# A quantised weight product and a feed-forward layer on one core: each codebook level summed in two 512-column halves, row products issued singly

## The chip, the core and the metric

The kernel runs on one core of one Trainium2 chip. The metric is the device time of one execution in microseconds (us).

## The reference

`x` is 4096 tokens (32 tiles of 128) by 2048. A weight matrix (2048 by 2048) is quantised with a codebook of 32 sorted entries, with a low-rank delta inside and outside the quantiser:

```python
lora_delta = lora_B @ lora_A * (LORA_ALPHA / LORA_RANK)        # rank 64
cb = codebook / jnp.clip(jnp.max(jnp.abs(codebook)), 1e-08)
normalized = ((weight + lora_delta).reshape(O, I // 128, 128)) / scale
idx = jnp.searchsorted((cb[:-1] + cb[1:]) * 0.5, normalized, side='left')
w_eff = (cb[idx] * scale).reshape(O, I) + lora_delta
c = x @ w_eff.T
result = jnp.einsum('bsd,od->bso', c, W_base) + b_base         # then a routed low-rank term
return x + result + mixed_term
```

The kernel multiplies the two weight matrices first (G = w_eff.T @ W_base.T, with 24 more columns for the router and the low-rank term, and the identity added for the residual) and then x @ G.

## The kernel before

**Tiles and groups.** The quantised matrix is worked on as 32 tiles q, each 128 partitions by 1024 columns, in buffers `wr`. Two tiles give one block of G's 16 row blocks, and four blocks make a group. The startup makes tiles 0 to 7, the first group. Then TensorE streams x through that group (`chunk`), makes the next group's G from tiles prepared meanwhile (`slot`), and so on. In this later part the work on tiles 8 to 31 goes on as background of ScalarE, VectorE and GpSimd, level by level between the evacuations.

**One tile.** The codebook has 31 steps. For each of them a mask is made by ScalarE (`ACT.Identity` with a huge scale, saturating into uint8: 0 or 255). For 24 levels (unit(q, j), j = 0 to 23) the mask `mk` is summed by VectorE into `acc`, which lies in PSUM over two banks; each sum reads the `acc` that the one before wrote and so waits for its end (semaphore `ac`). For the 7 other levels the mask `mp` goes to GpSimd, which scales it into `tm` (L1302) and adds it into `pp` (L1315). The places of these seven in ScalarE's order are j = 0, 1, 3, 6, 10, 13, 16 in the startup. The first level subtracts the normalised weight in `acc` (L1111), and GpSimd's first add starts from the same weight, so it cancels. VectorE closes the tile into `wr` (L1122, semaphore `cl`), GpSimd scales it and adds the delta (`effective`, L1323 and L1325, semaphore `we`). GpSimd also normalises the next tile (L1288, L1291). There are five mask buffers, so ScalarE can run five levels ahead of VectorE.

**TensorE in the startup.** When a tile is effective, its rows of G are summed by eight row products of five matmuls each (L703, fp32), each with one row tile of W_base that SP loads into three buffers (L511); the load for a product waits for the product three before it. `rows(q - 1)` issues the eight in one piece behind unit(q, 7). Delta products (L682 and L683) for coming tiles go through the single PSUM bank `pd`: each waits until the one before has been copied out to `ds` (semaphore `dl`), by ScalarE (L906) in unit order, the first four by VectorE (L1099). Places of delta products are `DELTA_AT`, a table of (q, j); there are 64, of which 36 lie in the startup. After tile 7 `final` multiplies its rows in another way (L722 on), after which the first `chunk` follows at once. At unit(q, 3) of tiles 3, 5, 7 `rows_out` copies the finished block of G (five ScalarE copies L957, five VectorE subtractions L1149).

**What sets the order.** `walk()` is one list of events. Each engine's program walks it and issues its own part of every event in that order; engines are bound to each other by semaphores alone. SP walks it too: a load or store that waits holds all that SP issues behind it.

Of the kernel before, what the change touches and what calls it, by code (L numbers as in the profile page):

```python
# [15 lines left out]
H = D // 2  # L16
# [64 lines left out]
def startup():  # L81
    for q in range(2 * N0):
        for j in range(NV):
            yield ("unit", q, j)
            if j == 7 and q:
                yield ("rows", q - 1)
            if j == 3 and q >= 3 and q % 2:
                yield ("rows_out", (q - 3) // 2)
# [110 lines left out]
class Room:  # L199
    def __init__(self, nc, ctx):  # L200
# [52 lines left out]
        self.dj = self.take("dj", NJ)  # L253
        self.sm = self.take("sm", 2)
# [109 lines left out]
def on_vector(n):  # L364

    return n < 4
# [7 lines left out]
def mask_places(q):  # L374

    return FIRST_AT if q == 0 else EARLY_AT if q < 2 * N0 else SPARE_AT

# [60 lines left out]
def book_steps(e, R, S):  # L438
# [17 lines left out]
    yield e.tensor_scalar(th, th, 0.5, None, ALU.mult).then_inc(bk, 1)  # L456
    yield e.tensor_tensor(dj, cn[:, 1:NC], cn[:, 0:NJ], ALU.subtract).then_inc(bk, 1)
    e.wait_ge(bk, 9)
# [16 lines left out]
BOOK_READY = 23  # L475


def sync_program(e, R, S, io, part, delta, out):
# [105 lines left out]
    for ev in walk():  # L584
# [17 lines left out]
        elif what == "rows":  # L602
            for r in range(8 * at[0] + 3, 8 * at[0] + 11):
                row(r)
            if at[0] == 2 * N0 - 3:
# [53 lines left out]
def tensor_program(e, R, S):  # L659
# [32 lines left out]
    def rows(q):  # L692
        b, h = q // 2, q % 2
        e.wait_ge(S["we"], q + 1)
        if q == 0:
            e.wait_ge(S["dl"], NARROW)
        for t in range(8 * h, 8 * h + 8):
            r = NB * b + t
            e.wait_ge(S[f"r{r % 3}"], 16 * (r // 3 + 1))
            for c in range(NCH):  # L700
                if t == 0 and b:
                    e.wait_ge(S["lo"], NCH * (b - 1) + c + 1)
                done = e.matmul(R.m[c][:, 0:width(c)], R.wr[raw_of(q)][:, (t % 8) * 128:(t % 8 + 1) * 128],  # L703
                                R.rows[r % 3][:, cols(c)], start=t == 0, stop=t == NB - 1 and not own(b, c))
            done.then_inc(S["row"], 1)
        if h:
# [129 lines left out]
    def turn(t):  # L836
# [3 lines left out]
        else:  # L840
            e.wait_ge(S["cl"], NQ)
# [12 lines left out]
    for ev in walk():  # L854
# [4 lines left out]
        elif what == "rows":  # L859
# [594 lines left out]
```

## Time and profile before

| | |
|---|---|
| device time, three runs | 2389.73 us median (2389.25 to 2390.38) |
| the profiled execution | span 2389.1 us from first to last instruction; its time is not listed apart from the three |
| TensorE, VectorE, ScalarE, GpSimd busy | 97%, 71%, 60%, 53% of the span |
| startup, until the first product of x | 339.1 us |

Busy time is an average over stages. The stages are told apart by windows, and what ends a wait by the rows of the timeline: a row's start, its duration, and in brackets how long the engine was idle ahead of it and for whom. Several alike instructions in a row are merged (x20), and their duration is that of the whole run; the time from one start to the next start is called the pitch here.

### The profile page before, as it was taken

The numbers are of one execution on the slowest core, as the hardware profiler recorded it, in microseconds if no ns is written. First come the engines' busy times: TensorE is split into PE (matmuls) and PEld (weight loads), VectorE is DVE, ScalarE is ACT, GpSimd is POOL, SyncE is SP. The second block draws the span as 40 slices with busy tenths as digits, with TensorE's granted clock in tenths as the row PEclk, the third lists the DMA queues.
The fourth block names the chain that finished last, engine by engine and source line by source line (L and its number), as shares of the span: only waits on it lengthen the run. The fifth ranks groups of instructions, "written<-read, shape, count | busy, mean of one in ns | idle before, by whom it ended". The sixth has DMA issues, their size and how long they took to land.

```text
span 2389.1 us, 30759 instructions
## 1 busy us (share of the span) xinstructions
PE 2318.9 (97%) x11678; PEld 2102.9 (88%) x11678; DVE 1708.0 (71%) x2021; ACT 1427.1 (60%) x1799; POOL 1270.6 (53%) x704
## 2 busy tenths in 40 slices
PE   3989899999999999999999999999999999999999
PEld 2445479999999999999999999999999989999998
DVE  8899998999978868777868967878873333333333
ACT  7999978989977656665646657566643321111111
POOL 6989847779874437777764436777760000111010
PEclk9989999999999999999999999999999999999999
DMA  5788854443343435766764436667664334545554
GB/s 198 272 274 277 309 208 162 162 166 141 138 149 114 118 116 197 238 230 225 234 219 123 119 105 200 222 232 238 221 208 128 102 96 161 197 180 198 185 195 152
DMA packets 121561, 442.58 MB, mean 185 GB/s; under 512 B 12818, under 2 KB 53330, under 8 KB 84562
## 3 DMA queue, kind: packets, MB, share of 16 engines
q1 hardware_dynamic: 121412, 440.61, 54.4%
q8 instruction: 92, 1.51, 0.3%
q14 instruction: 57, 0.47, 0.1%
HBM read 289.43 MB, written 151.13 MB: 184 GB/s over the span
## 4 chain that ended last, share of the span: by engine, by line
PE 91%; DVE 4%; ACT 3%; POOL 1%; issue 0%; DMA 0%; SPq 0%; DVEq 0%; POOLq 0%; ACTq 0%
PE m L777 20%; PE m L776 20%; PE m L778 20%; PE m L761 8%; PE m L762 8%; PE m L760 8%; PE m L703 4%; DVE acc L1115 3%; ACT mk L918 2%; PE m L806 1%; ACT mp L924 1%; PE pd L682 0%; DMA lb<-in_lb 0%; PE pd L683 0%; ACT ds L906 0%
## 5 line engine op out<-in xcount | busy, mean ns | idle before, releaser
L1115 DVE SCALAR_TENSOR_TENSOR acc<-mk,dj,acc 128x1024 f32<-128x1024 uint8 x736 | 944.9, 1284 | 91.6 <-ACT mk L918 72.1
L776 PE MATMUL m<-gh,xh 128*128 128x384 f32 (+2 forms) x2560 | 903.2, 353 | 0.0
L777 PE MATMUL m<-gl,xh 128*128 128x384 f32 (+2 forms) x2560 | 898.7, 351 | 0.0
L778 PE MATMUL m<-gh,xl 128*128 128x384 f32 (+2 forms) x2560 | 896.0, 350 | 0.0
L918 ACT ACTIVATE mk<-wr,bj 128x1024 uint8<-128x1024 f32 x768 | 843.8, 1139 | 0.7 <-DVE acc L1115 0.7
L776 PEld LDWEIGHTS m<-gh,xh 128*128 128x128 f32 x2560 | 481.6, 188 | 23.5
L778 PEld LDWEIGHTS m<-gh,xl 128*128 128x128 f32 x2560 | 480.9, 188 | 23.6
L777 PEld LDWEIGHTS m<-gl,xh 128*128 128x128 f32 x2560 | 481.4, 188 | 21.2
L1315 POOL TENSOR_TENSOR pp<-pp,tm 128x1024 f32<-128x1024 f32 x192 | 466.4, 2429 | 22.0
L1335 POOL TENSOR_TENSOR xl<-xw,xh 128x512 fp32r<-128x512 f32 x96 | 124.1, 1294 | 564.7 <-ACT xh L972 564.4
L1302 POOL TENSOR_SCALAR tm<-mp,dj 128x1024 f32<-128x1024 uint8 x224 | 258.1, 1152 | 246.5 <-ACT mp L924 235.6
L760 PE MATMUL m<-kh,wh 128*128 128x384 f32 (+2 forms) x936 | 328.8, 351 | 0.0
L762 PE MATMUL m<-kh,wl 128*128 128x384 f32 (+2 forms) x936 | 328.2, 351 | 0.0
L761 PE MATMUL m<-kl,wh 128*128 128x384 f32 (+2 forms) x936 | 328.0, 350 | 0.0
L1169 DVE TENSOR_TENSOR kl<-kw,kh 128x384 fp32r<-128x384 f32 (+2 forms) x234 | 189.1, 822 | 141.2 <-ACT kh L952 140.7
L1163 DVE TENSOR_TENSOR part<-m,part 128x384 f32<-128x384 f32 (+2 forms) x320 | 187.9, 587 | 131.5 <-PE m L778 130.4
L952 ACT ACTIVATE kh<-kw 128x384 fp32r<-128x384 f32 (+2 forms) x234 | 126.8, 548 | 251.8 <-DMA kw<-in_wb 251.2
L924 ACT ACTIVATE mp<-wr,bj 128x1024 uint8<-128x1024 f32 x224 | 255.1, 1139 | 0.1
L972 ACT ACTIVATE xh<-xw 128x512 fp32r<-128x512 f32 x128 | 80.1, 628 | 240.2 <-DMA xw<-in_x 240.2
L703 PE MATMUL m<-rows,wr 128*128 128x384 f32 (+2 forms) x560 | 207.6, 534 | 2.3 <-POOL wr L1325 1.5
L703 PEld LDWEIGHTS m<-rows,wr 128*128 128x128 f32 x560 | 112.2, 201 | 96.3 <-issue 50.6
L760 PEld LDWEIGHTS m<-kh,wh 128*128 128x128 f32 x936 | 175.8, 188 | 8.4 <-POOL wl L1329 0.2
(131 smaller groups left out, 1781.3 us busy)
## 6 DMA issues: line engine op xcount, KB each, us to landing
part<-part SPq DMA_DIRECT2D x192, 1036.0 KB, 6.7
rows<-in_wb SPq DMA_DIRECT2D x61, 1036.0 KB, 4.8
xw<-in_x SPq DMA_DIRECT2D x128, 256.0 KB, 3.2
out<-part SPq DMA_DIRECT2D x31, 1024.0 KB, 4.2
kw<-in_wb SPq DMA_DIRECT2D x138, 192.0 KB, 2.4
wr<-in_w SPq DMA_DIRECT2D x32, 512.0 KB, 8.8
dl<-delta SPq DMA_DIRECT2D x30, 512.0 KB, 5.9
delta<-ds SPq DMA_DIRECT2D x24, 512.0 KB, 3.2
```

Of the source, the lines that this page charges most:

```text
L703: done = e.matmul(R.m[c][:, 0:width(c)], R.wr[raw_of(q)][:, (t % 8) * 128:(t % 8 + 1) * 128], R.rows[r % 3][:, cols(c)], start=t == 0, sto ...
L760: e.matmul(bank[:, 0:w], high, kh, start=t == 0, stop=False)
L761: e.matmul(bank[:, 0:w], high, kl, start=False, stop=False)
L762: done = e.matmul(bank[:, 0:w], low, kh, start=False, stop=t == NB - 1 and not own(b, c))
L776: e.matmul(R.m[c][:, 0:w], xh, gh, start=k == 0, stop=False)
L777: e.matmul(R.m[c][:, 0:w], xh, gl, start=False, stop=False)
L778: done = e.matmul(R.m[c][:, 0:w], xl, gh, start=False, stop=stop and k == n - 1)
L918: e.activation(R.mk[k % NM], w, ACT.Identity, bias=R.bj[:, j:j + 1], scale=GROW).then_inc(S["mk"], 1)
L924: e.activation(R.mp[k % 2], w, ACT.Identity, bias=R.bj[:, NV + i:NV + i + 1], scale=GROW).then_inc(S["mp"], 1)
L1115: e.scalar_tensor_tensor(R.acc, R.mk[k % NM], R.dj[:, j:j + 1], R.acc, ALU.mult, ALU.add).then_inc(S["ac"], 1)
L1302: e.tensor_scalar(R.tm[scaled_level(q, i)], R.mp[k % 2], R.dj[:, NV + i:NV + i + 1], 0.0, ALU.mult, ALU.add).then_inc(S["tm"], 1)
L1315: e.tensor_tensor(R.pp, R.pp if i else R.wr[raw_of(q)], R.tm[scaled_level(q, i)], ALU.add).then_inc(S["pp"], 1)
```

## The change

Each level is summed in two halves of 512 columns, one instruction each, where a half waits only for the same half of the level before. The first level is no longer masked by ScalarE: VectorE compares the normalised weight itself (`is_gt`) and multiplies by the first codebook step. The weight no longer enters `acc` and `pp`; GpSimd's first mask is scaled with the lowest codebook entry added, and its next add starts from two `tm`, which makes six adds for seven. The tile is closed in two halves. `effective` waits for the close itself and no more for the first level of the next tile.

The eight row products become eight events behind units 7, 10, 15, 17, 20, 23, 23, 23 and the delta products of tiles 3 to 7 stand behind units 9, 14, 19, 23. The second and fourth of them are copied out by VectorE, the others by ScalarE. Tile 1 now has eight delta products (six before), tile 2 none (two before).

```diff
@@ -25,9 +25,12 @@
 NJ = NC - 1
 NP = 7
 NV = NJ - NP
+NA, MK = NP - 1, NV - 1
+HALVES = (slice(0, H // 2), slice(H // 2, H))
 SPARE_AT = (0, 3, 6, 10, 13, 16, 19)
 FIRST_AT, EARLY_AT = (1, 3, 5, 8, 11, 14, 17), (0, 1, 3, 6, 10, 13, 16)
 NORM_AT, SPLIT_EVERY = 8, 6
+ROW_AT, LATE_UNITS = (7, 10, 15, 17, 20, 23, 23, 23), (9, 14, 19, 23)
 GROUP = (4, 4, 4, 4)
 FINAL_ROW = NB * GROUP[0] - NB // 2
 CUT = (0, 384, 768, 1152, 1664, DX)
...
@@ -345,8 +350,8 @@
 
 def delta_places():
 
-    late = [(0, j) for j in range(6, 22, 2)] + [(1, j) for j in range(1, 7)] + [(2, 3), (2, 4)]
-    late += [(q, j) for q in range(3, 2 * N0) for j in range(3, 7)]
+    late = [(0, j) for j in range(6, 22, 2)] + [(1, j) for j in (1, 2, 3, 4, 5, 6, 9, 14)]
+    late += [(q, j) for q in range(3, 2 * N0) for j in LATE_UNITS]
     late += [(q, j) for q in range(2 * N0, NQ) for j in range(5, NV, 3)]
     return dict(zip(late, range(NDELTA)))
 
@@ -363,7 +368,7 @@
 
 def on_vector(n):
 
-    return n < 4
+    return n < 4 or 16 <= n < 16 + 4 * (2 * N0 - 3) and n % 2 == 1
 
 
 def unit_at(n):
...
@@ -599,10 +610,9 @@
-        elif what == "rows":
-            for r in range(8 * at[0] + 3, 8 * at[0] + 11):
-                row(r)
+        elif what == "row":
+            row(8 * at[0] + 3 + at[1])
...
@@ -908,14 +918,15 @@
                      scale=0.5).then_inc(S["dl"], 1)
 
     def unit(q, j):
-        k, w = NV * q + j, R.wr[raw_of(q)]
+        m, w = MK * q + j - 1, R.wr[raw_of(q)]
         if j == 0:
             e.wait_ge(S["n"], q + 1)
             if q == 0:
                 e.wait_ge(S["bk"], BOOK_READY)
-        if k >= NM:
-            e.wait_ge(S["ac"], k - NM + 1)
-        e.activation(R.mk[k % NM], w, ACT.Identity, bias=R.bj[:, j:j + 1], scale=GROW).then_inc(S["mk"], 1)
+        else:
+            if m >= NM:
+                e.wait_ge(S["ac"], summed((m - NM) // MK, (m - NM) % MK + 1))
+            e.activation(R.mk[m % NM], w, ACT.Identity, bias=R.bj[:, j:j + 1], scale=GROW).then_inc(S["mk"], 1)
         if j in mask_places(q):
             i = mask_places(q).index(j)
             k = NP * q + i
...
@@ -1100,32 +1111,36 @@
     def unit(q, j):
-        k = NV * q + j
-        if q >= 2 * N0 or k == 0:
-            e.wait_ge(S["mk"], k + 1)
-        elif j % 2:
-            e.wait_ge(S["mk"], k + 1 + (j < NV - 1))
-        if j == 0:
-            if q:
-                e.wait_ge(S["cl"], q)
-            e.scalar_tensor_tensor(R.acc, R.mk[k % NM], R.dj[:, j:j + 1], R.wr[raw_of(q)], ALU.mult,
-                                   ALU.subtract).then_inc(S["ac"], 1)
...
+        w, m = R.wr[raw_of(q)], MK * q + j - 1
+        for h, at in enumerate(HALVES):
+            if j == 0:
...
+                if q:
+                    e.wait_ge(S["cl"], 2 * q - 1 + h)
+                e.tensor_scalar(R.acc[:, at], w[:, at], R.u[:, 1:2], R.d0, ALU.is_gt, ALU.mult).then_inc(S["ac"], 1)
+                continue
...
+            e.wait_ge(S["ac"], summed(q, j - 1) - 1 + h)
+            e.scalar_tensor_tensor(R.acc[:, at], R.mk[m % NM][:, at], R.dj[:, j:j + 1], R.acc[:, at], ALU.mult,
                                    ALU.add).then_inc(S["ac"], 1)
         if j == NV - 1:
...
+                e.tensor_tensor(w[:, at], R.acc[:, at], R.pp[:, at], ALU.add).then_inc(S["cl"], 1)
...
@@ -1359,25 +1381,33 @@
         elif what == "effect":
-            if at[0] < 2 * N0:
+            if at[0] < 2 * N0 - 1:
                 spare_scaled(at[0] + 1, 0)
-            if at[0] < 2 * N0 - 1:
                 spare_scaled(at[0] + 1, 1)
-            if at[0] != 2 * N0 - 1:
+            if at[0] == 2 * N0 - 1:
+                spare_base(2 * N0)
+            else:
                 effective(*at)
```

The order of instructions, read from the two programs, not from a run. First TensorE between the row products of tile 4 (`wr_53`) and of tile 5 (`wr_54`), before:

```order
L703 MATMUL m<-rows_107,wr_53 128x408
L682 MATMUL pd<-las,lbh 128x512 [waits s_dl]
L683 MATMUL pd<-las,lbl 128x512
L682 MATMUL pd<-las,lbh 128x512 [waits s_dl]
L683 MATMUL pd<-las,lbl 128x512
L682 MATMUL pd<-las,lbh 128x512 [waits s_dl]
L683 MATMUL pd<-las,lbl 128x512
L682 MATMUL pd<-las,lbh 128x512 [waits s_dl]
L683 MATMUL pd<-las,lbl 128x512
L703 MATMUL m<-rows_108,wr_54 128x384 [waits d_r1,s_we]
```

Tile 4 in the program after, from the end of its first row product to its fifth:

```order
L713 MATMUL m<-rows_109,wr_53 128x408 [waits s_lo]
L692 MATMUL pd<-las,lbh 128x512 [waits s_dl]
L693 MATMUL pd<-las,lbl 128x512
...
L713 MATMUL m<-rows_107,wr_53 128x408
L692 MATMUL pd<-las,lbh 128x512 [waits s_dl]
L693 MATMUL pd<-las,lbl 128x512
...
L713 MATMUL m<-rows_108,wr_53 128x408
...
L713 MATMUL m<-rows_109,wr_53 128x408
L692 MATMUL pd<-las,lbh 128x512 [waits s_dl]
L693 MATMUL pd<-las,lbl 128x512
```

The four delta products stood together between two bursts of eight row products; now the first three stand behind the first, second and fourth row product of a tile, and the fourth behind the fifth.

VectorE at the end of tile 4, before:

```order
L1115 SCALAR_TENSOR_TENSOR acc<-mk_143,dj,acc 128x1024 [waits s_ac,s_mk]
L1115 SCALAR_TENSOR_TENSOR acc<-mk_144,dj,acc 128x1024 [waits s_ac]
L1115 SCALAR_TENSOR_TENSOR acc<-mk_145,dj,acc 128x1024 [waits s_ac,s_mk]
L1122 SCALAR_TENSOR_TENSOR wr_53<-acc,cn,pp 128x1024 [waits s_pp,s_mk,s_ac]
L1111 SCALAR_TENSOR_TENSOR acc<-mk_141,dj,wr_54 128x1024 [waits s_cl]
L1115 SCALAR_TENSOR_TENSOR acc<-mk_142,dj,acc 128x1024 [waits s_ac,s_mk]
L1115 SCALAR_TENSOR_TENSOR acc<-mk_143,dj,acc 128x1024 [waits s_ac]
```

and after:

```order
L1130 SCALAR_TENSOR_TENSOR acc<-mk_143,dj,acc 128x512 [waits s_ac,s_mk]
L1130 SCALAR_TENSOR_TENSOR acc<-mk_143,dj,acc 128x512 [waits s_ac]
L1130 SCALAR_TENSOR_TENSOR acc<-mk_144,dj,acc 128x512 [waits s_ac] x2
L1130 SCALAR_TENSOR_TENSOR acc<-mk_145,dj,acc 128x512 [waits s_ac,s_mk]
L1130 SCALAR_TENSOR_TENSOR acc<-mk_145,dj,acc 128x512 [waits s_ac]
L1137 TENSOR_TENSOR wr_53<-acc,pp 128x512 [waits s_ac,s_pp]
L1137 TENSOR_TENSOR wr_53<-acc,pp 128x512 [waits s_ac]
L1110 TENSOR_SCALAR ds_84<-pd 128x4x128 [waits s_pd]
L1123 TENSOR_SCALAR acc<-wr_54,u,d_158 128x512 [waits s_cl,s_n]
L1123 TENSOR_SCALAR acc<-wr_54,u,d_158 128x512 [waits s_cl]
L1130 SCALAR_TENSOR_TENSOR acc<-mk_141,dj,acc 128x512 [waits s_ac,s_mk]
L1130 SCALAR_TENSOR_TENSOR acc<-mk_141,dj,acc 128x512 [waits s_ac]
L1130 SCALAR_TENSOR_TENSOR acc<-mk_142,dj,acc 128x512 [waits s_ac] x2
```

Each level is two instructions that wait for different counts of `ac`, the close is two, and a copy of a delta product (L1110) stands behind it.

SP in tile 7, from the load of the next delta (`dl`), before:

```order
L496 DMA delta<-ds_83 128x4x256 [waits s_dl]
L505 DMA dl_136<-delta 128x1024 [waits d_ds2,s_we,d_ds1,d_ds0]
L496 DMA delta<-ds_84 128x4x256 [waits s_dl]
...
L511 DMA rows_107<-in_wb 128x2072 [waits s_row]
L511 DMA rows_108<-in_wb 128x2072 [waits s_row]
```

and after:

```order
L516 DMA dl_136<-delta 128x1024 [waits d_ds2,s_we,d_ds1,d_ds0]
L522 DMA rows_107<-in_wb 128x2072 [waits s_row]
L522 DMA rows_108<-in_wb 128x2072 [waits s_row]
L507 DMA delta<-ds_83 128x4x256 [waits s_dl]
L522 DMA rows_109<-in_wb 128x2072 [waits s_row]
L522 DMA rows_107<-in_wb 128x2072 [waits s_row]
L522 DMA rows_108<-in_wb 128x2072 [waits s_row]
L507 DMA delta<-ds_84 128x4x256 [waits s_dl]
...
L522 DMA rows_109<-in_wb 128x2072 [waits s_row]
L522 DMA rows_107<-in_wb 128x2072 [waits s_row]
L522 DMA rows_108<-in_wb 128x2072 [waits s_row]
```

A store of deltas, which waits for VectorE's copy behind the close of tile 7, now stands ahead of the last three row loads; those three bring the tiles for `final`.

## Rows read from the trace of the kernel before

**Rows 1.** The page, part 2: TensorE's busy tenths in 40 equal slices.
```profile
PE   3989899999999999999999999999999999999999
```

**Rows 2.** Windows by stage: busy us per engine, PEclk the granted clock.
```profile
66.65:314.80 248.15, 224.89 (x611) 120.75 (x609) 231.76 (x190) 236.52 (x249) 219.91 (x122) 0.94 0.83 288
314.80:340.00 25.20, 25.20 (x117) 21.23 (x118) 23.17 (x18) 19.51 (x18) 4.49 (x3) 1.00 0.58 218
340.00:700.00 360.00, 360.00 (x1907) 342.45 (x1907) 331.77 (x291) 326.37 (x402) 288.45 (x147) 1.00 0.42 148
```

**Rows 3.** Timeline of VectorE: start, us, engine, line, operation, count.
```profile
56.02 1.28 DVE L1122 SCALAR_TENSOR_TENSOR wr<-acc,cn,pp 128x1024 f32<-128x1024 f32 x1
...
207.80 1.29 DVE L1115 SCALAR_TENSOR_TENSOR acc<-mk,dj,acc 128x1024 f32<-128x1024 uint8 x1 [1.52 <-ACT mk L918]
209.00 2.57 DVE L1149 TENSOR_TENSOR gl<-m,gh 128x384 fp32r<-128x384 f32 x5
211.48 27.12 DVE L1115 SCALAR_TENSOR_TENSOR acc<-mk,dj,acc 128x1024 f32<-128x1024 uint8 x20
...
312.01 1.28 DVE L1122 SCALAR_TENSOR_TENSOR wr<-acc,cn,pp 128x1024 f32<-128x1024 f32 x1
313.33 0.69 DVE L1129 TENSOR_TENSOR wr<-wr,sc 128x512 f32<-128x512 f32 x1
314.06 0.69 DVE L1131 TENSOR_TENSOR wr<-wr,dl 128x512 f32<-128x512 f32 x1
314.66 0.68 DVE L1132 TENSOR_TENSOR wr<-wr,sc 128x512 f32<-128x512 f32 x1
...
321.04 2.31 DVE L1145 TENSOR_TENSOR gl<-fr,rh 128x2072 fp32r<-128x2072 f32 x1
323.27 2.31 DVE L1145 TENSOR_TENSOR rl<-rows,rh 128x2072 fp32r<-128x2072 f32 x1
```

**Rows 4.** Timeline of ScalarE; in brackets the idle time ahead of the instruction.
```profile
40.24 0.60 ACT L906 ACTIVATE ds<-pd 128x512 f32<-128x512 f32 x1 [1.64 <-PE pd L683]
...
49.44 4.26 ACT L918 ACTIVATE mk<-wr,bj 128x1024 uint8<-128x1024 f32 x4
...
204.11 0.60 ACT L906 ACTIVATE ds<-pd 128x512 f32<-128x512 f32 x1 [0.43 <-PE pd L683]
204.60 2.14 ACT L957 ACTIVATE gh<-m 128x384 fp32r<-128x384 f32 x5
206.58 1.19 ACT L918 ACTIVATE mk<-wr,bj 128x1024 uint8<-128x1024 f32 x1
...
299.50 8.41 ACT L918 ACTIVATE mk<-wr,bj 128x1024 uint8<-128x1024 f32 x8
```

**Rows 5.** Timeline of GpSimd in tile 5.
```profile
203.65 1.90 POOL L1323 TENSOR_TENSOR wr<-wr,sc 128x1024 f32<-128x1024 f32 x1 [1.64 <-DVE acc L1111]
...
207.92 2.37 POOL L1315 TENSOR_TENSOR pp<-wr,tm 128x1024 f32<-128x1024 f32 x1
210.46 1.12 POOL L1302 TENSOR_SCALAR tm<-mp,dj 128x1024 f32<-128x1024 uint8 x1 [0.17 <-POOL pp L1315]
...
230.07 4.79 POOL L1315 TENSOR_TENSOR pp<-pp,tm 128x1024 f32<-128x1024 f32 x2
```

**Rows 6.** Timeline of TensorE, startup.
```profile
66.65 30.52 PE L703 MATMUL m<-rows,wr 128*128 128x384 f32 x80
...
112.02 17.66 PE L703 MATMUL m<-rows,wr 128*128 128x384 f32 x50 [0.77 <-DMA rows<-in_wb]
...
284.60 29.08 PE L703 MATMUL m<-rows,wr 128*128 128x384 f32 x80
314.80 7.23 PE L722 MATMUL m<-rows,wr 128*128 128x384 f32 x20 [1.12 <-DVE wr L1131]
```

**Rows 7.** Windows around the start of a burst of row products.
```profile
210.00:215.00 5.00, 4.78 (x8) 2.85 (x9) 4.86 (x7) 5.00 (x7) 4.66 (x4) 0.50 0.80 247
```

**Rows 8.** The page, part 6: issue to landing of one row tile.
```profile
rows<-in_wb SPq DMA_DIRECT2D x61, 1036.0 KB, 4.8
```

More of the change, by code:

```diff
@@ L84, in startup @@
             yield ("unit", q, j)
-            if j == 7 and q:
-                yield ("rows", q - 1)
+            for k in range(8):
+                if ROW_AT[k] == j and q:
+                    yield ("row", q - 1, k)
             if j == 3 and q >= 3 and q % 2:
@@ L253, in __init__ @@
         self.dj = self.take("dj", NJ)
+        self.d0 = self.take("d0", 1)
         self.sm = self.take("sm", 2)
@@ L376, in mask_places, with summed @@
     return FIRST_AT if q == 0 else EARLY_AT if q < 2 * N0 else SPARE_AT
+def summed(q, j):
+    return 2 * (NV * q + j + 1)
 def scaled_level(q, i):
@@ L690, in one, with row @@
         return e.matmul(bank[:, o:o + 128], R.idn, R.idn, start=False, stop=True)
[L692 to L695, printed above, removed]
-            e.wait_ge(S["dl"], NARROW)
[L697 to L706, printed above, removed]
+    def row(q, k):
+        b, t = q // 2, 8 * (q % 2) + k
+        r = NB * b + t
+        if k == 0:
+            e.wait_ge(S["we"], q + 1)
+        if q == 0 and k == 0:
+            e.wait_ge(S["dl"], NARROW)
+        e.wait_ge(S[f"r{r % 3}"], 16 * (r // 3 + 1))
+        for c in range(NCH):
+            if t == 0 and b:
+                e.wait_ge(S["lo"], NCH * (b - 1) + c + 1)
+            done = e.matmul(R.m[c][:, 0:width(c)], R.wr[raw_of(q)][:, k * 128:(k + 1) * 128],
+                            R.rows[r % 3][:, cols(c)], start=t == 0, stop=t == NB - 1 and not own(b, c))
+        done.then_inc(S["row"], 1)
+        if t == NB - 1:
             if b == 0:
@@ L858, in tensor_program @@
                 wide(DELTA_AT[at])
-        elif what == "rows":
-            rows(*at)
+        elif what == "row":
+            row(*at)
         elif what == "final":
@@ L1291, in normalise, with spare_base @@
         e.tensor_tensor(grouped(w, 8), grouped(w, 8), per_group(R.rs, 8 * q, 8), ALU.mult).then_inc(S["n"], 1)
+    def spare_base(q):
+        e.wait_ge(S["mp"], NP * q + 1)
+        e.wait_ge(S["cl"], 2 * q)
+        e.tensor_scalar(R.pp, R.mp[NP * q % 2], R.dj[:, NV:NV + 1], R.cn[:, 0:1], ALU.mult, ALU.add).then_inc(S["tm"], 1)
     def spare_scaled(q, i):
@@ L1298, in spare_scaled @@
         if q >= 2 * N0:
[L1299 to L1302 removed]
+            e.wait_ge(S["pp"], NA * q + i - 1)
+        elif i in (2, 3):
+            e.wait_ge(S["pp"], NA * q + 1)
+        elif i > 3:
+            e.wait_ge(S["pp"], NA * q + i - 2)
+        elif q:
+            e.wait_ge(S["pp"], NA * q + i - 1)
+        e.tensor_scalar(R.tm[scaled_level(q, i)], R.mp[k % 2], R.dj[:, NV + i:NV + i + 1], 0.0 if i else R.cn[:, 0:1],
+                        ALU.mult, ALU.add).then_inc(S["tm"], 1)
     def spare_added(q, i):
         k = NP * q + i
[L1306 to L1307 removed]
+        if i == 1:
             if q:
[L1309 removed]
+                e.wait_ge(S["cl"], 2 * q)
             if q == 2 * N0:
                 e.wait_ge(S["rl"], NB // 2 - FINAL_WHOLE)
[L1312 to L1313 removed]
+        else:
+            e.wait_ge(S["pp"], NA * q + i - 1)
         e.wait_ge(S["tm"], k + 1)
[L1315 removed]
+        first = R.tm[scaled_level(q, 0)] if i == 1 and q < 2 * N0 else R.pp
+        e.tensor_tensor(R.pp, first, R.tm[scaled_level(q, i)], ALU.add).then_inc(S["pp"], 1)
     def effective(q):
         w = R.wr[raw_of(q)]
[L1319 to L1322 removed]
+        e.wait_ge(S["cl"], 2 * q + 2)
         e.tensor_tensor(grouped(w, 8), grouped(w, 8), per_group(R.sc, 8 * q, 8), ALU.mult).then_inc(S["ws"], 1)
```

73 lines of the change are left out of this document (36 added, 37 removed).

## The prediction

> **What bounds the kernel now.** I read the page's 40 slices first: TensorE is at nine tenths or more in nearly all slices behind the first six [rows 1]. The windows by stage make that sharp: from 314.8 to 340 us and from there to 1780 us TensorE is busy all the time, at clock 1.00 [rows 2]; the two stages of 540 us behind 700 us show the same. Nothing that the other engines do there can shorten it, only lengthen it. Between 66.65 and 314.80 TensorE is busy for 224.9 of 248.2 us, at a mean clock of 0.94 [rows 2]. So the change is worth what it moves the start of tile 7's final products, 314.80 us [rows 6].
>
> What bounds the startup is seen in the timelines. VectorE sums 20 levels in 27.12 us with no idle time: pitch (27.12 - 1.28) / 19 = 1.36 us, though the instruction itself takes 1.28 [rows 3]. That is a dependent pitch: where a level is followed by something that does not need its result, the next starts after 1.20 us (207.80 to 209.00). 24 levels and a close (1.32) make 33.9 us a tile; tiles 3, 5 and 7 have 2.48 us of low parts besides (209.00 to 211.48) [rows 3], so 36.4. The eight tiles close at 56.02 and 312.01, seven periods of 36.57 us [rows 3]. ScalarE is as full: masks at a pitch of (8.41 - 1.13) / 7 = 1.04 us, 31 a tile = 32.2, four delta copies at 0.49 (204.11 to 204.60) and on odd tiles five copies of G, 1.98 us (204.60 to 206.58) [rows 4]: 34.2 or 36.2 us. Both engines set the pace, and each alone would hide the other's gain.
>
> **The change, part by part.**
>
> VectorE, halves. A half is not in the trace. What stands nearest is 512 columns that wait for nothing late: 0.60 us from start to start (314.06 to 314.66), and 0.73 where it does wait for the one ahead (313.33 to 314.06) [rows 3]. Two halves of different banks alternate, so a half's input ended 0.5 us before it is needed: 2 x 0.60 = 1.20 a level. Upper bound: one op of 2072 columns takes 2.23 us (321.04 to 323.27), five with the same columns take 2.48 [rows 3], so a column costs 1.05 ns and an instruction 0.06 us; a level of 1024 takes 1.20, which is 0.13 over its columns. If that 0.13 is paid by each half, a level is 2 x (0.536 + 0.13) = 1.33. I take 1.20, as the five short ones read PSUM too and show no such surplus. A tile is then 24 x 1.20 + 1.20 = 30.0, with two delta copies 31.2, on odd tiles 33.7. From below nothing is faster than columns alone: 25.8.
>
> The Trainium skill ("VectorE: DVE Perf Modes", The TRN2 errata) charges a PSUM-source instruction 120 + columns cycles at 0.96 GHz, 0.66 us a half, an estimate of 1.32 a level: by it nearly all of VectorE's gain is gone. The same page of the Trainium skill (The DRAIN you can't avoid) says that a semaphore between chained instructions costs nothing; the trace does not agree, as the dependent pitch is 0.12 to 0.16 us longer at 1024 columns.
>
> ScalarE. One mask less: 30 x 1.04 = 31.2. Two delta copies in tiles 3 to 7 (1.0), eight in tile 1 (3.9), none in tile 2. The copies of G stay (2.0 in tiles 3, 5, 7), and so does a rounding of a new part of lora_A in tiles 1 and 6, 512 columns like a delta copy, taken as 0.5. So tiles 1 to 7 are 35.6, 31.2, 34.2, 32.2, 34.2, 32.7, 34.2: 234.3 us. VectorE has 7 x 30.0 + 10 x 0.6 + 3 x 2.5, about 224. ScalarE is now the bound, and VectorE follows it closely rather than five levels behind. Its own sum before was 246.4 (7 x 32.2, 28 delta copies, 3 x 2.0, 1.0), and its last masks of tile 0 and of tile 7 end at 49.44 + 3 x 1.04 = 52.6 and 299.50 + 7 x 1.04 = 306.8 [rows 4]: 254.2, so 7.8 went in waits, mostly for delta products that stood ahead of or behind 30 us of rows. I keep 3.5 of them.
>
> Tile 0. ScalarE waits 1.64 us for a delta product at 40.24 [rows 4], which waits for VectorE's copy of the one before; with one mask less and earlier sums I set the last mask at 50.0 in place of 52.6. So the last mask of tile 7 ends at 50.0 + 234.3 + 3.5 = 287.8, and the close, one level and two halves later, at 290.3, against 313.3. `Final_weights` takes two dependent halves (1.5) behind one delta copy (0.6): 292.4.
>
> GpSimd. From 203.65, the start of `effective`, to the end of its last add at 230.07 + 4.79 = 234.86 it needs 31.2 us; the add that is dropped takes 2.5 with its wait (207.92 to 210.46) [rows 5]. 28.7 and two scalings of the next tile (2.2) are 30.9, less than any ScalarE tile but tile 2, which is equal. `effective` stands behind the second scaling, whose mask ScalarE makes as its third of the next tile: it starts 3 x 1.04 + 1.1 = 4.2 us after ScalarE begins that tile, some 1.8 after the close. It takes 4.3 (203.65 to 207.92) [rows 5], so row products start 6.1 after the close.
>
> TensorE. Eight products take 28.3 us at full clock (17.66 for five, 3.53 each), but the bursts before take 29.1 to 30.5 [rows 6], because the clock is at 0.50 from 210 to 215 us, after a stretch with only delta products and gaps, which opens a burst [rows 7]. With delta products between row products no such stretch is left, and I count 3.53 each. A delta product is at most 0.9, the share of 512 columns in 3.53. That work alone, 28.3 + 3.6, fits in 33 us. But the order ties it to ScalarE: the fourth delta product waits for ScalarE's copy behind level 19, and the last three row products stand behind it. In tile 7 that is 26 masks (27.0), G's copies 2.0, two delta copies 1.0, and 0.25 of wait behind the tile's start at 287.8 - 34.7 = 253.1: 283.3. With 0.9 for the product and 10.6 for three rows, TensorE is free at 294.8. That is later than 292.4.
>
> SP. The loads for the final products stand behind the store of the last deltas, which waits for VectorE's copy behind the close (290.3 + 0.6). A row tile takes 4.8 us from issue to landing [rows 8]: 295.7, and a little more behind the store, which has half its bytes. I set the start of the final products at 297.0 for 314.8: 17.8 us.
>
> Later stages. From 340 to 700 us VectorE is busy 331.8 of 360 us [rows 2], the fullest place. Its levels were 1.28 of busy time and become 1.20; ScalarE and GpSimd lose one mask and one add a tile. I cost this at nothing, under TensorE's full time. The cover ends if a level costs 0.15 us more than now (28.2 us idle over 188 levels, eight tiles less the four of tile 8 that lie ahead).
>
> **Rivals.** (a) TensorE and SP are tied to the copies more tightly than I summed: a row load that stands behind a store, a product behind a late copy, 1 to 2 us in each tile, which then delays G's copies on ScalarE. For it: SP's order. Against it: the slack of 1 to 2 us in most tiles. Price 7 x 1.3 = 9 us of 17.8: 2381. (b) The fixed cost of 0.13 is paid by every half. VectorE then needs 33.4 + 1.3 a tile and 2.5 on odd ones, as before: 2387 to 2390, no change. The five short instructions that cost 0.06 each speak against it [rows 3]. The Trainium skill's rule on fixed cost, cited above, leads to this case. (c) Slower: each half waits on a semaphore and pays the dependent 0.73 though its input is long there. A level is then 1.46, 0.10 over now; with close and copies a tile is 2.5 to 4 longer, some 20 us in all, 2410, and from 340 to 700 us the level is 0.18 over its busy time now, more than the 0.15 that VectorE's idle time there can take. It decides from 1.36 a level on. Against it: the low parts each wait for ScalarE's copy, which has come, and still start at the short pitch [rows 3]. (d) The gain is larger: no wait is left on ScalarE and the row tile for the final products is early, start at 290: 2365 or a little less.
>
> **How the numbers follow.** The page's span is 2389.1 and the runs' median 2389.73, so a shift of 17.8 gives 2371.3 and 2371.9. I forecast 2372. Chances: this case 0.70, within 2365 to 2379; (a) 0.12, 2379 to 2386; (b) 0.06; (c) 0.07; (d) 0.05. A range from 2364 to 2384 leaves out (c), most of (b) and the ends of (a) and (d), about 2 in 10. What a measurement can tell from no change is about 0.2%, 4.8 us, so faster is the first case, most of (a), (d): 0.86; the same 0.06 and slower 0.08.
>
> **What would show it.** Halves at a pitch of 0.60 in the startup, and VectorE idle for ScalarE's masks; tile closes 32 to 36 us apart, the last at 288 to 292; PEclk near 1.00 from 100 us on; the first final product at 295 to 299, waiting for a row tile or for rows of tile 6; TensorE still without a gap from there to 1780 us. I am wrong if halves start 0.67 or more apart, if the clock still falls between tiles, or if TensorE shows gaps after 340 us.

## The result: slower, and the profile after

The change takes 2408.77 us (median of 4 runs, 2407.05 to 2410.87) against 2389.88 for the kernel before beside it: a ratio of 1.0079, 95% interval 1.0065 to 1.0094. The forecast was 2372, so the sign was wrong. The profiled span is 2405.3 us for 2389.1; it is that of the fastest of the four runs (2407.05). Two executions among all those below took 9005 us (the kernel before) and 9730 us (the kernel with copies and stores both moved) and are left out.

The windows of the change, with the columns of [rows 2]: the startup, and a long stretch behind it.

```profile
66.65:330.65 264.00, 222.53 (x608) 119.92 (x607) 245.34 (x372) 225.78 (x233) 202.63 (x114) 0.94 0.74 267
...
340.00:1240.00 900.00, 900.00 (x4777) 857.06 (x4776) 771.52 (x1134) 654.80 (x783) 572.54 (x313) 1.00 0.51 171
```

From 340 to 1780 us TensorE has no gap, as before, and behind 1780 it is idle for 4.4 us, for 4.3. Nearly everything is lost ahead of 340: the first final product starts at 330.65 us for 314.80 [rows 6], 15.9 us later, and the span is 16.2 longer. TensorE was busy 222.5 us of that stretch for 224.9 (its first row product started at 64.46, 2.2 us ahead of the window), but stood idle 41.5 us of it for 23.3. The granted clock did not rise, 0.94 in both.

VectorE's timeline in tiles 4 and 5:

```profile
201.43 1.28 DVE L1137 TENSOR_TENSOR wr<-acc,pp 128x512 f32<-128x512 f32 x2
202.63 0.68 DVE L1110 TENSOR_SCALAR ds<-pd 128x512 f32<-128x512 f32 x1
203.23 1.52 DVE L1123 TENSOR_SCALAR acc<-wr,u,d 128x512 f32<-128x512 f32 x2
204.66 2.72 DVE L1130 SCALAR_TENSOR_TENSOR acc<-mk,dj,acc 128x512 f32<-128x512 uint8 x4
212.21 1.42 DVE L1130 SCALAR_TENSOR_TENSOR acc<-mk,dj,acc 128x512 f32<-128x512 uint8 x2 [4.83 <-ACT mk L929]
213.53 2.57 DVE L1164 TENSOR_TENSOR gl<-m,gh 128x384 fp32r<-128x384 f32 x5
216.02 14.57 DVE L1130 SCALAR_TENSOR_TENSOR acc<-mk,dj,acc 128x512 f32<-128x512 uint8 x22
230.50 0.68 DVE L1110 TENSOR_SCALAR ds<-pd 128x512 f32<-128x512 f32 x1
231.10 11.93 DVE L1130 SCALAR_TENSOR_TENSOR acc<-mk,dj,acc 128x512 f32<-128x512 uint8 x18
242.95 1.28 DVE L1137 TENSOR_TENSOR wr<-acc,pp 128x512 f32<-128x512 f32 x2
244.15 0.68 DVE L1110 TENSOR_SCALAR ds<-pd 128x512 f32<-128x512 f32 x1
```

22 halves without idle time take (230.50 - 216.02) / 22 = 0.658 us each, so a level takes 1.32 us where 1.36 stood [rows 3] and 1.20 was forecast. The two halves of the close take 0.60 each (201.43 to 202.63) and those of the comparison 0.71 (203.23 to 204.66). A tile without copies is 23 x 1.317 + 1.43 + 1.20 = 32.9 us; tile 2 is exactly that (closes at 93.35 and 126.28). The other closes lie 37 to 41.5 us apart, and the last is at 320.82 for 312.01. In the tile of the rows above 41.52 us lie between the closes: 32.9, two copies (1.2), the low parts (2.5) and 4.83 us of idle time. To find the origin of that idle time the other queues are read at the same place. SP:

```profile
189.69 0.38 SPq L507 DMA_DIRECT2D delta<-ds  x1
190.11 4.18 SPq L522 DMA_DIRECT2D rows<-in_wb  x3
203.34 0.38 SPq L507 DMA_DIRECT2D delta<-ds  x1
203.77 5.33 SPq L522 DMA_DIRECT2D rows<-in_wb  x3
...
231.21 0.38 SPq L507 DMA_DIRECT2D delta<-ds  x1
231.63 4.18 SPq L522 DMA_DIRECT2D rows<-in_wb  x3
244.85 0.38 SPq L507 DMA_DIRECT2D delta<-ds  x1
245.27 3.60 SPq L522 DMA_DIRECT2D rows<-in_wb  x3
```

Each store leaves within 0.1 us of the end of VectorE's copy (they start at 188.98, 202.63, 230.50 and 244.15 and take 0.68 us each) and three row loads follow each. TensorE and ScalarE:

```profile
196.35 12.39 PE L713 MATMUL m<-rows,wr 128*128 128x384 f32 x30 [1.96 <-DMA rows<-in_wb]
208.58 0.38 PE L700 MATMUL m<-idn 128*128 128x128 f32 x2
214.23 5.23 PE L713 MATMUL m<-rows,wr 128*128 128x384 f32 x10 [5.27 <-DVE gl L1164]
...
237.81 10.70 PE L713 MATMUL m<-rows,wr 128*128 128x384 f32 x30 [1.90 <-DMA rows<-in_wb]
251.55 5.34 PE L713 MATMUL m<-rows,wr 128*128 128x384 f32 x10 [3.04 <-DMA rows<-in_wb]
256.42 0.71 PE L692 MATMUL pd<-las,lbh 128*128 128x512 f32 x1
```
```profile
209.00 2.15 ACT L968 ACTIVATE gh<-m 128x384 fp32r<-128x384 f32 x5 [5.57 <-PE m L700]
211.00 3.25 ACT L929 ACTIVATE mk<-wr,bj 128x1024 uint8<-128x1024 f32 x3
...
257.40 0.60 ACT L916 ACTIVATE ds<-pd 128x512 f32<-128x512 f32 x1 [4.49 <-PE pd L693]
```

This is a ring of four queues (VectorE, SP, TensorE, ScalarE), each of which runs its own instructions in the order of the program. VectorE's copy at level 14 ends at 189.7; the store and the loads follow; TensorE's last three row products of the tile start at 196.35, having waited 1.96 us for their row tile, and the product that closes the block ends at 209.0. ScalarE, with G's copies next in its queue, has stood idle 5.57 us for them and starts its next mask at 211.00; VectorE has stood idle 4.83 us for that mask. On the other kind of tile the link is the delta product: the loads behind the close's store come at 245.27, the tile's first row product waits until 251.55, the delta product behind it runs at 256.42, and ScalarE, whose copy stands ahead of its masks, starts it at 257.40 after 4.49 us. VectorE is late again (2.28 us of idle time ahead of its level at 259.07), so its next copy is. The page's median for a row load is 6.6 us to landing, for 4.8 [rows 8]; why a load takes longer was not tested, and it is not the loss by itself, as the median is 6.1 in a kernel below that takes the time of before.

### The profile page after: what moved, and what is told of

The parts are those of the page before. It is cut to its first block, busy times and chain, and to the rows that moved or that the text cites. A ratio compares the mean times of both kernels' runs of the same rounds, so it can differ in the third digit from the quotient of the medians.

```text
span 2405.3 us, 31470 instructions
## 1 busy us (share of the span) xinstructions
PE 2319.0 (96%) x11678; PEld 2102.9 (87%) x11678; DVE 1758.0 (73%) x2832; ACT 1390.6 (58%) x1757; POOL 1178.4 (49%) x672
## 4 chain that ended last, share of the span: by engine, by line
PE 88%; ACT 5%; DVE 4%; DMA 2%; issue 1%; SPq 0%; POOL 0%; DVEq 0%; ACTq 0%
PE m L787 20%; PE m L786 20%; PE m L788 20%; PE m L770 8%; PE m L771 8%; PE m L772 8%; DVE acc L1130 3%; ACT mk L929 3%; PE m L713 2%; DMA rows<-in_wb 1%; ACT mp L935 1%; PE m L816 1%; PE pd L692 0%; PE pd L693 0%; ACT ds L916 0%
## 5 line engine op out<-in xcount | busy, mean ns | idle before, releaser
L1130 DVE SCALAR_TENSOR_TENSOR acc<-mk,dj,acc 128x512 f32<-128x512 uint8 x1472 | 1018.3, 748 | 86.0 <-ACT mk L929 84.1
L929 ACT ACTIVATE mk<-wr,bj 128x1024 uint8<-128x1024 f32 x736 | 809.4, 1139 | 3.1 <-DVE acc L1130 2.5
L1340 POOL TENSOR_TENSOR pp<-pp,tm 128x1024 f32<-128x1024 f32 x184 | 447.1, 2430 | 22.3 <-POOL tm L1326 0.6
L1326 POOL TENSOR_SCALAR tm<-mp,dj 128x1024 f32<-128x1024 uint8 x192 | 217.7, 1134 | 295.0 <-ACT mp L935 290.9
L713 PE MATMUL m<-rows,wr 128*128 128x384 f32 (+2 forms) x560 | 215.2, 542 | 37.5 <-DMA rows<-in_wb 17.5
```

The costliest lines, as they stand in the source:

```text
L713: done = e.matmul(R.m[c][:, 0:width(c)], R.wr[raw_of(q)][:, k * 128:(k + 1) * 128], R.rows[r % 3][:, cols(c)], start=t == 0, stop=t == NB ...
L929: e.activation(R.mk[m % NM], w, ACT.Identity, bias=R.bj[:, j:j + 1], scale=GROW).then_inc(S["mk"], 1)
L1130: e.scalar_tensor_tensor(R.acc[:, at], R.mk[m % NM][:, at], R.dj[:, j:j + 1], R.acc[:, at], ALU.mult, ALU.add).then_inc(S["ac"], 1)
L1326: e.tensor_scalar(R.tm[scaled_level(q, i)], R.mp[k % 2], R.dj[:, NV + i:NV + i + 1], 0.0 if i else R.cn[:, 0:1], ALU.mult, ALU.add).then_i ...
L1340: e.tensor_tensor(R.pp, first, R.tm[scaled_level(q, i)], ALU.add).then_inc(S["pp"], 1)
```

## Experiments

The kernel before ran beside every one at 2389.7 to 2390.6 us.

**One half level by itself.** Series on VectorE alone, output replaced by a copy of x (no part of the computation).

> No part of the computation: x is copied to the output, and VectorE runs short series of 512-column instructions by themselves. Pitches expected: if a fixed cost per scalar_tensor_tensor sets the 0.66 us, series on eight banks with no wait are at 0.66 too, and whole levels without a wait at 1.20; if the met semaphore wait costs it, those without a wait are at 0.60 and those with a met wait at 0.66; if PSUM on both sides costs it, the ones with one side in SBUF are at 0.60; if the uint8 mask, the f32 mask is at 0.60; if the pointer scalar, the immediate is at 0.60.

Timeline of VectorE; each row is one series. L60: two halves in turn, each waiting for its own sum. L64: the same op on eight banks, no wait. L69: a wait long met. L73: an f32 mask in place of the byte mask. L77: immediate in place of the scalar from memory. L81: no PSUM. L93: `tensor_tensor` on PSUM. L101: whole levels without, L106 with a wait for the one before. L110 and L114: the comparison with two scalars from memory, and with immediates.

```profile
15.99 10.63 DVE L60 SCALAR_TENSOR_TENSOR ps<-mk,sc,ps 128x512 f32<-128x512 uint8 x16
26.66 5.37 DVE L64 SCALAR_TENSOR_TENSOR ps<-mk,sc,ps 128x512 f32<-128x512 uint8 x8
32.06 5.37 DVE L69 SCALAR_TENSOR_TENSOR ps<-mk,sc,ps 128x512 f32<-128x512 uint8 x8
37.46 5.37 DVE L73 SCALAR_TENSOR_TENSOR ps<-fm,sc,ps 128x512 f32<-128x512 f32 x8
42.86 4.88 DVE L77 SCALAR_TENSOR_TENSOR ps<-mk,ps 128x512 f32<-128x512 uint8 x8
47.77 5.39 DVE L81 SCALAR_TENSOR_TENSOR sb<-mk,sc,sb 128x512 f32<-128x512 uint8 x8
...
64.03 4.88 DVE L93 TENSOR_TENSOR ps<-ps,fm 128x512 f32<-128x512 f32 x8
...
73.86 4.86 DVE L101 SCALAR_TENSOR_TENSOR ps<-mk,sc,ps 128x1024 f32<-128x1024 uint8 x4
78.82 7.91 DVE L106 SCALAR_TENSOR_TENSOR ps<-mk,sc,ps 128x1024 f32<-128x1024 uint8 x6
86.77 5.81 DVE L110 TENSOR_SCALAR ps<-w,sc 128x512 f32<-128x512 f32 x8
92.62 4.84 DVE L114 TENSOR_SCALAR ps<-w 128x512 f32<-128x512 f32 x8
```

A half takes 0.66 us from start to start in L60, L64, L69, L73 and L81: (5.37 - 0.75) / 7, with 0.75 as the length of one. It takes 0.60 in L77 and L93: (4.88 - 0.69) / 7. L110 takes 0.71, L114 0.59. Each scalar that is read from memory costs 0.06 us per instruction, and neither a wait for something that has already ended, nor PSUM, nor the byte mask costs anything. A whole level takes 1.19 free and 1.32 behind its own sum: (7.91 - 1.29) / 5. Two halves save that wait (0.13) and pay one more instruction with its scalar (0.13, which is 2 x 0.66 - 1.19): 1.32 for 1.32. In the kernel itself a whole level behind its own sum takes 1.36, so that two halves do save 0.04 there; where that 0.04 comes from is open.

The Trainium skill ("VectorE: DVE Perf Modes", The TRN2 errata) charges an instruction that reads PSUM 120 cycles and one per column, an estimate of 0.66 us for such a half, and the number agrees. Its reason, PSUM as the source, does not: the same columns of PSUM without the scalar take 0.60, and without PSUM, with the scalar, 0.66. What the same page of the Trainium skill says of chained instructions, that a semaphore costs nothing extra (The DRAIN you can't avoid), holds for a wait that is met (L69), not for one on the instruction just ahead (L106).

**Sums and order apart.** First the new sums in the old order, then the old sums in the new order.

```diff
-ROW_AT, LATE_UNITS = (7, 10, 15, 17, 20, 23, 23, 23), (9, 14, 19, 23)
+ROW_AT, LATE_UNITS = (7,) * 8, (3, 4, 5, 6)
...
-    return n < 4 or 16 <= n < 16 + 4 * (2 * N0 - 3) and n % 2 == 1
+    return n < 4
```

> The halves, the compare and the six adds of the change, but row products in one piece behind unit 7, delta products of tiles 3 to 7 behind units 3 to 6 and all but four copies on ScalarE, as before. Theory 1 (the order made it slow: row loads on SP stand behind delta stores that wait for VectorE, and ScalarE, TensorE and SP wait for each other in a ring): with the ring gone a level is 1.32 us for 1.36, the close and the first level as in the trace after, a tile 33 us and 35.5 on odd tiles against 33.9 and 36.4 before, and 2 us saved in tile 0: 2379 us, from 2374 to 2384. Theory 2 (the halves made it slow: twice the instructions cost VectorE time in the startup and later): 2400 to 2410, as the change itself.

> The kernel before with the new places of row and delta products and the copies on VectorE, but whole levels, 31 masks and seven adds. Theory 1 (the order is the cause): slower than before by 15 to 30 us, 2405 to 2420, with TensorE waiting for row tiles 2 us or more before the sixth row product of each tile from 3 on. Theory 2 (the halves): 2385 to 2394.

The sums alone: 2386.59 (ratio 0.9985, 0.9976 to 0.9994), outside the 2374 to 2384 that was expected of them. The order alone, with whole levels, all masks and seven adds: 2415.23 (1.0105, 1.0090 to 1.0120). The order, in which the copies on VectorE are included, is the loss: 25 us with the old sums and 22 with the new ones. The sums give 3.5 us in the old order and 6.5 in the new one.

**Halves and comparison apart.** The comparison and the six adds with whole levels, in either order (`HALVES = (slice(0, H),)`, counts of `cl` and `ac` to match).

> The six-add sums and the comparison with whole levels of 1024 columns, in the order of before (no halves). Theory A, that two halves cost as much as one dependent whole level (measured by themselves: a pair of halves 1.32 us, a dependent whole one 1.33 us), and that the gain of the halves in the old order (2386.6) came from the comparison and the sum that is left out: levels at 1.33 us, closes within 0.5 us of that run's, 2385 to 2389. Theory B, that the halves carried the gain: the time of before, 2390 (2389 to 2391).

> The change with whole levels of 1024 columns (comparison, six adds, new order, copies as in the change). Halves give 1.317 us a level and whole dependent ones 1.33. Theory A, the halves matter as little here as in the order of before: 2407 to 2412. Theory B, a half lets the copies and the low parts in between start sooner and takes part in the ring: over 2413.

2386.91 (0.9986, 0.9976 to 0.9995) and 2410.81 (1.0085, 1.0070 to 1.0100). The halves are worth 0.3 us in one order and about 2 in the other, within the scatter of the runs. What gains in the old order is the comparison, with the mask, the add and the wait for the first mask that are gone; these were not taken apart.

That does not mean that VectorE gains nothing by the halves. Whole levels in the old order:

```profile
135.05 27.13 DVE L1131 SCALAR_TENSOR_TENSOR acc<-mk,dj,acc 128x1024 f32<-128x1024 uint8 x20
```

This is 1.36 us a level, (27.13 - 1.29) / 19, for 1.32 with halves. Between its first and its last close VectorE works 247.8 us with whole levels and 243.1 with halves, but waits 4.7 us for masks in the first kernel and 10.3 in the second: what the halves save is spent waiting for ScalarE. This is what the prediction said of two engines that both set the pace, each hiding the other's gain.

**The stores.** SP's stores of tiles 3 to 7 behind the third and behind the eighth row load; then only one of them.

```diff
-                if n % 2:
+                if n % 2 and 3 <= q < 2 * N0:
+                    late_store = n
+                elif n % 2:
                     delta_out(n)
...
             row(8 * at[0] + 3 + at[1])
+            if late_store is not None and at[1] in (2, 7):
+                delta_out(late_store)
+                late_store = None
```

> The change, with only SP's delta stores of tiles 3 to 7 moved: the first of a tile behind its third row load, the second behind the eighth. Theory 1 in its narrow form (the store ahead of the loads closes the ring): the waits for row tiles (17.5 us in the startup) fall under 5 us, the first final product comes 8 to 15 us earlier than 330.65, and the kernel takes 2394 to 2401 us. Wide form (ScalarE's copy at level 9 behind the first row product, and the low parts of G, tie it by themselves): 2403 to 2408. Theory 2 (the halves): 2408, no change.

> The change, with only the store of the first pair of deltas of tiles 3 to 7 (SyncE, level 14) put behind the third row load; the one behind the close stays. Moving both saved 16.7 us. Theory A, each store delays its own row loads: the waits for rows behind the first store are about 2 us in each of five tiles, so about 8 to 10 us of the 16.7 come back, 2400 (2397 to 2402). Theory B, the ring holds unless both go: 0 to 3 us, 2406 to 2409. Theory C, either one alone opens the ring: 2392 to 2395.

> The change, with only the store behind the close of tiles 3 to 7 put behind the eighth row load; the one at level 14 stays. Theory A: the waits of 3.0 us for rows before a tile's fourth row product in two tiles, and what hides behind the waits for the low parts of m in the others, 6 to 9 us back, 2401 (2399 to 2404). Theory B, the ring holds unless both go: 2406 to 2409. Theory C, either alone opens it: 2392 to 2395.

Both: 2392.03 (1.0009, 0.9999 to 1.0018), 16.7 us less than the change and 2 less than the lowest expected; between 130 and 330 us no row product waits for a row tile any more. The first alone: 2408.81 (1.0077, 1.0062 to 1.0092), nothing. The second alone: 2402.83 (1.0052, 1.0037 to 1.0067), 6 us. The savings do not add up, 0 and 6 for 16.7: with one store moved, row products still wait for row tiles behind the other, 15.0 us with the first moved and 11.7 with the second, for 16.6 in the change (130 to 330 us).

**The copies.** The change with all delta copies of tiles 3 to 7 on ScalarE (`return n < 4`), the stores where the change has them; the same with the stores moved too; and the reverse, VectorE's copies put into the old order with the new sums.

> The change with all delta copies of tiles 3 to 7 on ScalarE (none on VectorE); the stores stay ahead of the row loads. Theory A, VectorE's copy is a link of the ring (SyncE's store waits for it, and it stands behind VectorE's levels; ScalarE's copy stands some 3 us ahead of them): the stores leave about 3 us earlier, ScalarE works 1.2 us more in a tile, some 9 us back over five tiles, 2399 (2395 to 2403). Theory B, ScalarE ends last, its ten more copies of 0.59 us come on top: 2411 to 2416. Theory C, VectorE's copies are nothing: 2407 to 2410.

> The same with the stores of tiles 3 to 7 behind the third and the eighth row load as well (that alone gave 2392.0). What is left of the change then are the halves, the comparison, the single row products and the places of the deltas. Theory A, the hand-over between VectorE and ScalarE by TensorE is the rest of the loss (ScalarE waited 11.8 us for delta products there): 2386 to 2389. Theory B, ScalarE's 5.9 us of copies come on top of what it waits now: 2394 to 2398.

> The halves in the order of before, with one in two of the delta copies of tiles 3 to 7 on VectorE and not on ScalarE (ten copies of 0.59 us leave ScalarE, ten of 0.68 us come to VectorE). Theory A, ScalarE ends last in tiles 3 to 7 (VectorE waited 13.1 us for masks there): about 0.6 us less wait per copy on some of them, 2382 (2380 to 2385). Theory B, VectorE ends last and the masks only look late: the copies lengthen its tile, 2388 to 2393.

2389.43 (0.9998, 0.9988 to 1.0007); 2390.50 (0.9999, 0.9990 to 1.0009); 2411.64 (1.0087, 1.0070 to 1.0104). The first missed its expectation of 2399 by 10 us, the second lies between its two, and the third is 18 us above its highest. Putting ten copies back on ScalarE takes away the whole loss against the kernel before, 19.3 us. Moving the stores alone took away 16.7, and with the copies on ScalarE it adds nothing: copies and stores are links of one chain, and it opens when either is moved. SP and VectorE in this kernel, tile 5:

```profile
221.77 0.38 SPq L507 DMA_DIRECT2D delta<-ds  x1
222.19 6.37 SPq L522 DMA_DIRECT2D rows<-in_wb  x3
233.12 0.38 SPq L507 DMA_DIRECT2D delta<-ds  x1
```
```profile
236.20 1.28 DVE L1137 TENSOR_TENSOR wr<-acc,pp 128x512 f32<-128x512 f32 x2
```

The store of level 23 now leaves 3.1 us ahead of the close (233.12 and 236.20), where in the change it leaves 1.9 behind (244.85 and 242.95), as ScalarE runs some levels ahead of VectorE and VectorE's copy stands behind everything that it sums. From 100 us on no row product of this startup waits for a row tile (0.6 us ahead of that; the first final product waits 2.3), while in the change they wait 17.5 us before the first final product; ScalarE's wait for delta products between 130 and 330 us falls from 15.4 to 6.0. The third kernel shows a second way to lose with the same copies, 25 us over the same sums without them, with next to no wait for a row tile (0.3 us between 130 and 330). TensorE, VectorE and ScalarE:

```profile
219.16 0.80 PE L692 MATMUL pd<-las,lbh 128*128 128x512 f32 x1 [8.17 <-DVE ds L1110]
```
```profile
217.10 1.41 DVE L1130 SCALAR_TENSOR_TENSOR acc<-mk,dj,acc 128x512 f32<-128x512 uint8 x2
218.41 0.69 DVE L1110 TENSOR_SCALAR ds<-pd 128x512 f32<-128x512 f32 x1
222.09 2.73 DVE L1130 SCALAR_TENSOR_TENSOR acc<-mk,dj,acc 128x512 f32<-128x512 uint8 x4 [2.98 <-ACT mk L929]
```
```profile
220.42 0.60 ACT L916 ACTIVATE ds<-pd 128x512 f32<-128x512 f32 x1 [6.12 <-PE pd L693]
```

ScalarE, in the last row, waits 6.12 us for a delta product. That product waits for VectorE's copy of the one before (`pd` is a single buffer), and the copy stands behind levels that themselves waited for ScalarE's masks (2.34 us ahead of 213.30). Then VectorE waits 2.98 us for ScalarE. ScalarE lost 34.8 us to such waits between 130 and 330 us.

**Which copy.** VectorE keeps only the copy of level 14, or only the one behind the close (`n % 4 == 1`, `n % 4 == 3`).

> The change with VectorE copying in tiles 3 to 7 only the delta product of level 14; the one behind the close is ScalarE's. With none on VectorE it was 2389.4, with both 2408.8. Theory A, the copy behind the close is the link that counts (SyncE's store, the loads of the last three row tiles and TensorE's first row product of the next tile follow it at once): 2389 to 2393. Theory B, each does its half: 2397 to 2401. Theory C, the one at level 14 counts: 2404 to 2409.

> The change with VectorE copying in tiles 3 to 7 only the delta product behind the close; the one of level 14 is ScalarE's. Theory A, the copy behind the close is the link that counts: 2403 to 2409. Theory B, each does its half: 2397 to 2401. Theory C: 2389 to 2393.

2399.55 (1.0039, 1.0025 to 1.0052) and 2407.60 (1.0073, 1.0058 to 1.0088). The copy behind the close alone costs 18 us over the kernel with none, that of level 14 alone 10, and both together 19. The first is what was expected if each copy does its half, the second what was expected if the one behind the close is all that counts; no single one of the three theories covers both, as all took the two costs for shares of one sum. In the close's kernel TensorE waits, at the place seen above, longer than in the change:

```profile
251.38 5.41 PE L713 MATMUL m<-rows,wr 128*128 128x384 f32 x10 [4.66 <-DMA rows<-in_wb]
```

**Three things around it.** G's copies at level 7 in place of 3, on top of the moved stores; the delta products of the old order at levels 0, 2, 4, 6; and the new sums in the old order with only the row products issued singly.

> The change with both stores behind row loads (2392.0), and ScalarE's and VectorE's copies of the five banks of m moved from level 3 to level 7 of tiles 3, 5 and 7. Theory A, TensorE's last row products come too late for level 3, ScalarE waits for them in front of its masks (9 us in three tiles in the change) and the low parts wait for ScalarE: ScalarE's wait goes, TensorE waits about 5 us longer three times but has that time, 2388 to 2390. Theory B, TensorE's wait for the low parts (17.8 us) grows by four levels each, 15 us, and pushes its delta products in front of ScalarE: 2396 to 2405.

> Whole levels with the comparison in the order of before (2386.9), with the four delta products and copies of tiles 3 to 7 at levels 0, 2, 4 and 6 for 3, 4, 5 and 6. Theory A, VectorE ends last there (it waited only 1.9 us for masks) and the spacing only empties TensorE's and ScalarE's waits for one another (17.1 and 6.9 us): 2385.5 to 2387.5. Theory B, these waits reach the end: 2381 to 2385. A third way, a delta product at level 0 stands ahead of TensorE's row products still to come from the tile before: later by 1 to 5 us.

> Halves, comparison and the order of before for the delta products and copies (2386.6), with the eight row products of a tile issued one by one at levels 7, 10, 15, 17, 20, 23, 23, 23 and not together at 7. The delta products of a tile stay ahead of all row products of the tile's own, so only SyncE's loads and TensorE's order against the delta products of the next tile can move. Theory A, nothing between rows and deltas changes and the time stays: 2385 to 2388. Theory B, loads of single rows behind the next deltas' stores, or rows behind the load of the next delta, cost something by themselves: 2390 to 2400.

2407.04 (1.0068, 1.0053 to 1.0083), 15 us over the kernel it was made from and 2 above the expected range: between 130 and 330 us TensorE waits 29.6 us for the low parts for 17.8, ScalarE 26.3 for delta products for 8.2, and VectorE 17.8 for masks for 3.0. 2387.13 (0.9985, 0.9976 to 0.9995), as with whole levels unspaced. But the spacing did not take TensorE's waits for ScalarE's copies away (17.1 us between 100 and 330 with it and without), so what these cost stays open. 2384.45 (0.9978, 0.9968 to 0.9987), just below the expected 2385 to 2388: single row products cost nothing, and this is the fastest kernel of the study, 5.3 us ahead of before. Its first final product starts at 309.77 us and its last close at 306.10; rows hold TensorE up for 0.5 us between 130 and 330.

This last kernel and the one with all copies on ScalarE (2389.43) differ in the places of the delta products alone: (3, 4, 5, 6) against (9, 14, 19, 23), with those of tiles 1 and 2. So spreading them over the tile costs 5 us by itself. Those 5 us, hidden in "the time of before", are a part of the change that gains nothing.

## Why the prediction was wrong

**VectorE, halves.** It took 1.20 a level and gave 1.33 as the upper bound; 1.317 was measured. The reason given for 1.20, that five short instructions on PSUM show no surplus, was true of them, but they read no scalar from memory. The bound held; the choice between the bounds did not. With 0.66 from half to half it also stayed just under the 0.67 that the prediction had set as the sign of being wrong.

**ScalarE, "I keep 3.5 of them".** This is the step that failed in sign: a wait of 3.5 us was 28.7. ScalarE's own work was sized right. From its last mask of tile 0 (it ends at 51.5, forecast 50.0) to its last of tile 7 (316.6, forecast 287.8) it was busy 236.2 us, for 234.3. In the same stretch it waited 17.1 us for delta products, 9.1 for the row products that G's copies need and 2.5 for a free mask buffer. The prediction followed the chain of copy, store, row load once, at tile 7, and not in the four tiles before it, where it feeds back.

VectorE shows what reached the tiles. The end of the last close moved from 290.3 in the forecast to 322.1, 31.8 us. Tile 0 closed 3.4 us later than its part of the sum (50.0 + 2.5). Between the two closes VectorE stood idle for masks 17.9 us (8.2 before), so it worked 266.2 - 17.9 = 248.3 us. That is 10.5 over the 237.8 that ScalarE was given (234.3 and 3.5), and 3.4, 17.9 and 10.5 are the 31.8. The 10.5 comes mostly from the halves' size: VectorE was given 224, and 0.117 us more on 7 x 23 levels are 18.9, part of which was to be hidden under ScalarE.

**SP.** At tile 7 the chain came as described, but took longer: the final products start 8.6 us behind the end of the close, for 6.7 forecast. Their row tile is issued at 323.70 and TensorE starts at 330.65, having waited for it. Against the kernel before, 8.8 of the 15.9 us lie ahead of the last close (320.82 for 312.01) and 7.0 behind it (9.8 us from the start of the close to the final product, for 2.8).

**TensorE.** "With delta products between row products no such stretch is left" failed too: the granted clock stayed at 0.94. It was 0.68 from 214.20 to 219.00, behind the 5.27 us wait for low parts, and 0.56 from 196.35 to 200.00, behind the wait of 1.96 us for a row tile, so that three row products took 12.39 us. But it was 1.00 from 237.80 to 241.00, behind a wait of 1.90 us, where the same three took 10.70. Which of these waits lower the clock is open. It was right that the work alone fits; the ties were the matter.

**GpSimd and the later stages.** GpSimd set no pace in the rows read: `effective` starts at 202.79, 0.1 us behind the close, for 1.8 forecast. In the later stages TensorE has no gap from 340 to 1780 us, as forecast. The reason was half right: VectorE's work there was to shrink, and grew, to 334.9 us of 360 from 340 to 700 for 331.8 [rows 2], which TensorE's full time still covers.

**Rivals.** (a) named the mechanism, SP's order and a product behind a late copy that delay G's copies, and priced it at 1.3 us a tile from the slack. The ten copies alone cost about 19 us over five tiles. That each late tile starts the next one late fits the rows, but was not measured tile by tile. It was also counted as a smaller gain and not as a loss. (b) gave the halves' true size. (c), the slower one, had the right time, 2410, for a reason that did not occur: a wait that is met costs nothing (L69). That its time fits is luck. (d) did not occur.

## What to carry to other kernels

Before an operation is moved to another engine, look at what is queued ahead of it there and which queues start behind it. Here ten copies of 0.6 us, moved from the engine that runs ahead to the one that closes the tile, cost 19 us in the new order, where a store, three row loads and the next products hang on each, and 25 in the old one, where only the next delta product does. A wait that feeds a later stage of its own chain is priced per round and carried on, not added once; a single experiment that moves the operation back finds it sooner than shares of its waits do. Splitting an instruction to hide its latency pays only if the latency is longer than the cost of one more instruction, and only as far as the engine that feeds it can follow.

## What the hardware showed unexpectedly

On VectorE a scalar operand from memory costs 0.06 us per instruction and per scalar (0.60, 0.66 and 0.71 us from start to start for 512 columns with none, one and two). PSUM as source or target of f32 costs nothing over SBUF at this size. A wait on the instruction just ahead costs 0.13 us at 1024 columns in the series (1.32 for 1.19) and 0.16 in the kernel (1.36 for 1.20), and one on the instruction before that nothing at 512 (L60 and L64).
